# A transformer-like kernel on one core: all hi one-hots of the expert scatter move from GpSimd to DVE, with new orders for PE, ACT and GpSimd and new PSUM banks

## What is computed

```python
x = _L0_conv_ref(x, ...)                 # per image: layernorm, q; strided 7x7 depthwise conv gives offsets;
                                         # bilinear sampling of x at 64 places; 8-head attention; MLP
t = _to_tokens(x)
t = t + _L1_attn_ref(_ln_t(t), ...)      # 8 heads, top 4 of 16 segments of 32 keys per query
t = t + _L1_ffn_ref(_ln_t(t), ...)       # experts chosen by product keys:
#   q  = layernorm(t @ Wq.T + bq) per head (8 heads of 64); two halves, l2norm
#   s0, s1 = scores against 64 + 64 keys; top 16 of each
#   fs, pos = top 16 of the 16 x 16 sums; ci = ix0 + ix1 is the expert (0..126)
#   inner = t . expert_down[fi]; out = sum(gelu(inner) * softmax(fs) * expert_up[fi])
```

## Time and profile before

| | |
|---|---|
| Three runs | 449.9, 451.67 (median), 452.0 us |
| The profiled execution | 449.87 us, its span 447.8 us |
| DVE busy | 358.4 us, 80% |
| PE busy | 308.1 us, 69% |
| POOL busy | 217.9 us, 49% |
| ACT busy | 140.7 us, 31% |
| Mean granted PE clock | 0.701 |

### The profile page before, as it was taken

One profiled execution on the slowest core, in us unless ns is written; L12 is line 12 of the kernel. 1 busy time (PEld: TensorE's weight loads), 2 busy tenths in 40 slices (PEclk: granted clock), 3 DMA queues, 4 the chain that ended last, 5 costly groups with the idle time before them and its releaser, 6 DMA issues.

```text
span 447.8 us, 7841 instructions
## 1 busy us (share of the span) xinstructions
PE 308.1 (69%) x2275; PEld 225.2 (50%) x2275; DVE 358.4 (80%) x2163; ACT 140.7 (31%) x324; POOL 217.9 (49%) x411
## 2 busy tenths in 40 slices
PE   2096558788119576799978778996556769850497
PEld 1044235456016344498855457974323359730494
DVE  1848238238999989799999979999997899999930
ACT  2125231655213147523224373033042241041000
POOL 6319932227935387796244937312073532085700
PEclk9997566898655678865685986568659576566556
DMA  6000000000000000000000000000000000000000
GB/s 222 0 0 1 1 1 0 1 1 1 1 1 0 1 2 1 1 1 1 2 1 1 1 13 1 2 0 3 1 1 12 0 1 2 2 0 12 2 1 12
DMA packets 1634, 3.50 MB, mean 8 GB/s; under 512 B 180, under 2 KB 1205, under 8 KB 1592
## 3 DMA queue, kind: packets, MB, share of 16 engines
q1 hardware_dynamic: 1592, 3.01, 1.9%
HBM read 2.49 MB, written 0.52 MB: 7 GB/s over the span
## 4 chain that ended last, share of the span: by engine, by line
DVE 55%; PE 23%; POOL 9%; issue 6%; ACT 6%; DMA 1%; DVEq 0%; ACTq 0%; POOLq 0%
PE bank L876 6%; DVE Sx L1363 5%; DVE i L1369 5%; DVE i L1370 5%; DVE cands L1419 4%; DVE onehot L494 4%; DVE vraw L1366 3%; DVE vraw L1360 3%; DVE segmax L1244 3%; DVE c L1416 3%; PE bank L540 2%; PE bank L550 2%; DVE masked L1426 2%; PE bank L783 2%; ACT hat L914 2%
## 5 line engine op out<-in xcount | busy, mean ns | idle before, releaser
L876 PEld LDWEIGHTS bank<-weights,onehot 108*128 108x128 f16 x1024 | 69.0, 178 | 3.1 <-DVE onehot L494 1.5
L876 PE MATMUL bank<-weights,onehot 108*128 108x16 f16 x1024 | 69.0, 216 | 1.9 <-DVE onehot L494 1.4
L1644 POOL TENSOR_TENSOR inv<-nrm,mhalf 128x16 f32<-128x16 f32 x8 | 23.4, 2925 | 35.8 <-DVE nrm L1376 35.8
L458 POOL TENSOR_TENSOR taps<-qpad,wa 128x128 f32<-128x128 f32 x96 | 36.0, 427 | 2.0 <-ACT qpad L929 1.9
L540 PE MATMUL bank<-wa,hat 128*128 128x128 f32 x24 | 6.7, 371 | 32.9 <-ACT hat L914 32.9
L1557 POOL TENSOR_TENSOR rstd<-veps,mhalf 128x2 f32<-128x2 f32 x16 | 11.7, 731 | 34.6 <-DVE veps L1166 34.3
L1370 DVE FIND_INDEX8 i<-vraw,Sx 128x8 uint16<-128x64 f32 x128 | 28.0, 219 | 0.0
L1369 DVE FIND_INDEX8 i<-vraw,S 128x8 uint16<-128x64 f32 x128 | 28.0, 218 | 0.0
L1363 DVE MATCH_REPLACE8 Sx<-vraw,S 128x64 f32<-128x64 f32 x128 | 25.1, 209 | 0.0
L803 PE MATMUL bank<-KB,qsT 128*128 128x256 f32 x64 | 24.9, 558 | 0.2 <-issue 0.2
L494 DVE TENSOR_SCALAR onehot<-eT 108x512 f16<-108x512 uint16 x84 | 24.4, 366 | 0.0
(11 more groups left out here) (228 smaller groups left out, 811.5 us busy)
## 6 DMA issues: line engine op xcount, KB each, us to landing
wa<-wa_dram SPq DMA_DIRECT2D x1, 747.5 KB, 4.9
wb<-wb_dram SPq DMA_DIRECT2D x1, 707.0 KB, 5.2
x_sb<-x_dram SPq DMA_DIRECT2D x4, 128.0 KB, 4.0
out_dram<-eT SPq DMA_DIRECT2D x4, 128.0 KB, 1.7
onehot<-ws_dram SPq DMA_DIRECT2D x1, 448.0 KB, 5.9
bq_row<-rows_dram SPq DMA_DIRECT2D x1, 0.5 KB
onehot<-rows_dram SPq DMA_DIRECT2D x1, 13.5 KB
```

The costliest lines, as they stand in the source:

```text
L458: ins = eng.tensor_tensor(tv[:, :, :, ky, kx:kx + n], q, dw[:, ky, kx:kx + n].unsqueeze(1).unsqueeze(1).broadcast_to([P, G8, G8, n]), ALU. ...
L876: last = mm(o[:, g * 16:g * 16 + 16], OHv[:, c * NT + t, g], Rv[:, c, t, g, s], start=(c == 0 and s == 0), stop=(c == NCH - 1 and s == 1))
L1644: g_.tensor_tensor(inv[:, n], nrm[:, n], mhalf[:, 0:2 * H], ALU.pow).then_inc(inv_ready, 1)
```

## The change

All 32 one-hots are DVE's. POOL's N3b and N3i and the semaphore onehot_pool_ready are gone. The orders of PE, ACT and POOL and the banks are new; DVE's order is the same. PE has 19 fillers in place of 21, at other places. In POOL's order only N3b and N3i are taken out. In the orders, cut to the parts spoken of below:

```diff
-POOL_HI = 4
...
     "tensor":
-    A1a.0 A2d.0 A1b.0 W.0 W.1 A3a.0 A3b.0 A3c.0 A4.0 W.2 W.3 F5a.0 A1a.1 F5c.0 NS.0 F6a.0 F6b.0 W.4 W.5
-    F6c.0 F7a.0 F7b.0 F8a.0 A1b.1 F8b.0 F9b.0 A2d.1 F9a.0 F9c.0 A3a.1 A3b.1 W.6 A3c.1 A4.1 W.7 W.8 F8c.0
-    F9d.0 W.9 F10a.0
+    A1a.0 A1b.0 A2d.0 A3a.0 A3b.0 A3c.0 A4.0 F5a.0 A1a.1 A1b.1 F5c.0 F6a.0 W.0 NS.0 F6b.0 F6c.0 F7a.0 F7b.0
+    F8a.0 W.1 W.2 F8b.0 F9b.0 F9a.0 A2d.1 F9c.0 A3a.1 A3b.1 A3c.1 A4.1 W.3 W.4 F9d.0 F8c.0 F10a.0
...
-    A4.2 F11a.1 F11t.1 F5a.2
+    F11a.1 A4.2 W.6 W.7 F11t.1 F5a.2
...
-    F11a.3 N6b.1 F11t.3 W.12 W.13 F11b.3 F11c.3 W.14 N3a.2 F12.3 N0a.3
+    F11a.3 F11t.3 W.10 W.11 N6b.1 F11b.3 F11c.3 W.12 N3a.2 W.13 W.14 W.15 W.16 F12.3 N0a.3
...
-    N5a.2 N0f.3 N0e.3 W.15 N5b.2 N0g.3 W.16 N6a.2 W.17 N4.3 N6b.2 N3a.3 N3h.3 N5a.3 W.18 N5b.3 W.19 W.20 N6a.3 N6b.3
+    N5a.2 W.17 N5b.2 W.18 N4.3 N6a.2 N6b.2 N3a.3 N3h.3 N5a.3 N5b.3 N6a.3 N6b.3
     "scalar":
-    F5b.0 A1a.1 F5c.0 F6b.0
+    F5b.0 A1a.1 A1b.1 F5c.0 F6b.0
...
-    F12.0 F5c.1 N0a.0 F6b.1 A1a.2 N0h.0 N0b.0 N0c.0
+    F12.0 F5c.1 N0a.0 N0h.0 F6b.1 N0b.0 N0c.0 A1a.2
...
-    F12.1 N4.0 F5c.2 N0a.1 N0h.1 A0b.3
+    F12.1 F5c.2 N0a.1 N4.0 A0b.3 N0h.1
...
-    N4.2 N0e.3 N2p.3 N2q.3 N6a.2 N4.3 N3a.3 N3h.3 N6a.3
+    N4.2 N0d.3 N0e.3 N6a.2 N2p.3 N2q.3 N3a.3 N3h.3 N4.3 N6a.3
...
@@ PE @@
             def N5a(b):
                 pe.wait_ge(onehot_dve_ready, b + 1)
-                pe.wait_ge(onehot_pool_ready, b + 1)
                 scatter(b, 0)
...
@@ DVE @@
             def N3b(b):
-                for hi in range(POOL_HI, HI):
+                for hi in range(HI):
                     last = masks(v, hi, first_halves(b))
                 last.then_inc(onehot_dve_ready, 1)
...
@@ POOL @@
-            def N3b(b):
-                if b >= 1:
-                    full(pool, "G1", b - 1)
-                pool.wait_ge(eT_ready, b + 1)
-                for hi in range(0, POOL_HI):
-                    last = masks(g_, hi, first_halves(b))
-                last.then_inc(onehot_pool_ready, 1)
```

More of the change, by code:

```diff
@@ L109 @@
 ORDERS = {
-    "tensor": """A1a.0 A2d.0 A1b.0 W.0 W.1 A3a.0 A3b.0 A3c.0 A4.0 W.2 W.3 F5a.0 A1a.1 F5c.0 NS.0 F6a.0 F6b.0 W.4 W.5
-        F6c.0 F7a.0 F7b.0 F8a.0 A1b.1 F8b.0 F9b.0 A2d.1 F9a.0 F9c.0 A3a.1 A3b.1 W.6 A3c.1 A4.1 W.7 W.8 F8c.0
[L112 to L129, removed]
+    "tensor": """A1a.0 A1b.0 A2d.0 A3a.0 A3b.0 A3c.0 A4.0 F5a.0 A1a.1 A1b.1 F5c.0 F6a.0 W.0 NS.0 F6b.0 F6c.0 F7a.0 F7b.0
+        F8a.0 W.1 W.2 F8b.0 F9b.0 F9a.0 A2d.1 F9c.0 A3a.1 A3b.1 A3c.1 A4.1 W.3 W.4 F9d.0 F8c.0 F10a.0 F10b.0
+        F11a.0 W.5 F11t.0 F5a.1 F11b.0 F11c.0 A1a.2 F5c.1 F12.0 N0a.0 F6a.1 N0h.0 F6b.1 N0b.0 F6c.1 N0c.0 N0f.0
+        N0d.0 F7a.1 F7b.1 N0e.0 F8a.1 F8b.1 N0g.0 F9b.1 F9a.1 A1b.2 F9c.1 A2d.2 F8c.1 A3a.2 F9d.1 A3b.2 A3c.2
+        F10a.1 F10b.1 F11a.1 A4.2 W.6 W.7 F11t.1 F5a.2 F11b.1 F11c.1 N3a.0 N4.0 F5c.2 F12.1 N0a.1 N0h.1 W.8
+        F6a.2 A1a.3 W.9 F6b.2 N0b.1 F6c.2 N0c.1 N0d.1 N0f.1 N5a.0 F7a.2 N0e.1 F7b.2 N5b.0 F8a.2 F8b.2 A2d.3
+        F9b.2 F9a.2 F9c.2 N0g.1 F8c.2 N6a.0 A1b.3 F9d.2 A3a.3 F10a.2 A3b.3 F10b.2 A3c.3 F11a.2 N4.1 A4.3 F11t.2
+        F5a.3 F11b.2 N6b.0 F11c.2 N3a.1 F5c.3 F12.2 N0a.2 N0h.2 F6a.3 F6b.3 N0b.2 F6c.3 N0c.2 N0f.2 N5a.1 N5b.1
+        F7a.3 N0d.2 F7b.3 N0e.2 N0g.2 F8a.3 F8b.3 F9b.3 F9a.3 F9c.3 N6a.1 F9d.3 N4.2 F10a.3 F10b.3 F8c.3 F11a.3
+        F11t.3 W.10 W.11 N6b.1 F11b.3 F11c.3 W.12 N3a.2 W.13 W.14 W.15 W.16 F12.3 N0a.3 N0h.3 N0b.3 N0c.3 N0f.3
+        N0d.3 N0g.3 N0e.3 N5a.2 W.17 N5b.2 W.18 N4.3 N6a.2 N6b.2 N3a.3 N3h.3 N5a.3 N5b.3 N6a.3 N6b.3""".split(),
@@ new lines @@
+    "scalar": """A0b.0 A1a.0 A2c.0 A2d.0 A1b.0 A3a.0 A3b.0 A3c.0 A4.0 A0b.1 F5b.0 A1a.1 A1b.1 F5c.0 F6b.0 F7a.0 F7b.0
+        F8a.0 A2c.1 F8b.0 A2d.1 F9a.0 A3a.1 A3b.1 A3c.1 F8c.0 A4.1 F10a.0 F10b.0 A0b.2 F11t.0 F11b.0 F5b.1 F12.0
+        F5c.1 N0a.0 N0h.0 F6b.1 N0b.0 N0c.0 A1a.2 F7a.1 N0d.0 F7b.1 N0e.0 F8a.1 F8b.1 N2p.0 A2c.2 F9a.1 A2d.2
+        A3a.2 F8c.1 A3b.2 A1b.2 N2q.0 A3c.2 F10a.1 F10b.1 F11t.1 A4.2 F11b.1 N3a.0 F5b.2 F12.1 F5c.2 N0a.1 N4.0
+        A0b.3 N0h.1 F6b.2 N0b.1 A1a.3 N0c.1 N0d.1 F7a.2 N0e.1 F7b.2 F8a.2 A2c.3 F8b.2 A2d.3 N2p.1 F9a.2 F8c.2
+        A3a.3 N6a.0 F10a.2 A3b.3 F10b.2 A1b.3 N2q.1 A3c.3 F11t.2 A4.3 F11b.2 F5b.3 N3a.1 F12.2 F5c.3 N0a.2 N0h.2
+        F6b.3 N0b.2 N0c.2 N4.1 F7a.3 N0d.2 F7b.3 N0e.2 F8a.3 F8b.3 N2p.2 F9a.3 F10a.3 F10b.3 N6a.1 F8c.3 N2q.2
+        F11t.3 F11b.3 N3a.2 F12.3 N0a.3 N0h.3 N0b.3 N0c.3 N4.2 N0d.3 N0e.3 N6a.2 N2p.3 N2q.3 N3a.3 N3h.3 N4.3
@@ L141 @@
         A2b.1 F8b.3 F7b.0 A2b2.1 A3a.1 A4.1 A0a.2 A0b.2 F11c.0 N0a.0 N0h.0 A2a.2 F6c.1 A2a2.2 A2b.2 A2b2.2 N0f.0
[L142 to L145, removed]
+        F7b.1 N2a.0 N0g.0 A3a.2 N2d.0 N2c.0 A4.2 N2f.0 F11c.1 A0a.3 A0b.3 N0a.1 N0h.1 A2a.3 F6c.2 A2a2.3 A2b.3
+        N0f.1 A2b2.3 F7b.2 N2a.1 A3a.3 N0g.1 N2d.1 A4.3 N2c.1 N2f.1 F11c.2 N0a.2 N0h.2 F6c.3 N0f.2 F7b.3 N2a.2
+        N2c.2 N0g.2 N2d.2 N2f.2 F11c.3 N0a.3 N0h.3 N0f.3 N0g.3 N2a.3 N2d.3 N2c.3 N2f.3""".split(),
 }
@@ L155, in schedule @@
     return out
[L158 to L161, removed]
+BANKS = """01234560132456013245601234560123452160163405234160523416052163462142314263052463
+         01524630152563015234601523460152341352605134023460512345162350164235601042352614
+         35261435206135213065126302563254106354120654143206514326143261430261430621406235
+         46210356201"""
 def place_jobs():
@@ L404, in build @@
         onehot_dve_ready = sem("onehot_dve_ready")
-        onehot_pool_ready = sem("onehot_pool_ready")
         out_ready = sem("out_ready")
@@ L865, in N5b @@
                     pe.wait_ge(onehot_dve_ready, b + 2)
-                    pe.wait_ge(onehot_pool_ready, b + 2)
                 scatter(b, 1)
@@ L1120, in N3a @@
                     ac.wait_ge(onehot_dve_ready, b)
-                    ac.wait_ge(onehot_pool_ready, b)
                     full(ac, "YT", b - 1)
@@ L1700, in N2f @@
                 merge(b, 1)
-            def N3b(b):
-                if b >= 1:
-                    full(pool, "G1", b - 1)
-                pool.wait_ge(eT_ready, b + 1)
-                for hi in range(0, POOL_HI):
-                    last = masks(g_, hi, first_halves(b))
-                last.then_inc(onehot_pool_ready, 1)
[L1710 to L1714, removed]
             do = {"A0a": A0a, "A0b": A0b, "A2a": A2a, "A2a2": A2a2, "A2b": A2b, "A2b2": A2b2, "A3a": A3a, "A4": A4, "F6c": F6c, "F7b": F7b,
                   "F11c": F11c, "NS": NS, "N0a": N0a, "N0h": N0h, "N0f": N0f, "N0g": N0g, "N2a":
-                  N2a, "N2c": N2c, "N2d": N2d, "N2f": N2f, "N3b": N3b, "N3i": N3i}
+                  N2a, "N2c": N2c, "N2d": N2d, "N2f": N2f}
             for s, b in schedule("gpsimd"):
```

## The result

The changed kernel took 444.5 us (median of 4 runs, 442.65 to 446.63) against 451.84 us (449.9 to 452.19) for the kernel before: ratio 0.9864, 95% interval [0.9833, 0.9895]. It is faster by 1.4%. The profiled execution took 442.65 us, its span 440.9 us, where before's took 447.8: 6.9 us less.

A forecast was written before the change was run, and what follows sets the result against it. DVE was taken to bound the kernel from about 105 to 429 us, a dependent chain before, PE after. Terms -5.6 - 1.0 - 1.46 + 0.5 - 0.6 + 0.3 + 0.8 = -7.1 us gave 444.5 us, range 439.5 to 449.5.

The forecast's parts named there:

- Port relief, images 0 to 2: DVE's 32 one-hots per image run faster with POOL quiet than 28 beside it: 5.6 us saved.
- rival D: Full blocking: each POOL one-hot stops DVE for its whole length, so relief is 16.1 us, total 434 us; chance 0.03.
- Tail one-hots: Image 3: 32 one-hots of 256 columns on DVE take 4.58 us instead of 5.59, 1.0 us saved.
- Tail fillers: PE fillers W.18 to W.20 leave the order around the last scatters: 1.46 us saved.
- The late exponential: Tail of image 3: ACT's N6a.2 ahead of N2p.3 delays the exponential and POOL's queue: 0.5 us lost, bounds 0 and 2.
- The seam of image 1: A4.2 and two fillers come ahead of F11t.1: 0.3 us lost, up to 1.
- I count 1.1 of the 1.52: Image 0: DVE's shorter work then waits for POOL's inverse root, so 1.1 of 1.52 us gained is kept.
- The seam of image 3: Fillers W.12 to W.16 about N3a.2 hold PE's clock for the queries: 0.6 us saved; 1.0 gained to 1.5 lost.
- The front: Image 0: new PE and ACT order, A1b.1 before F5c.0, outcome depending on PE's clock: 0.8 us lost.
- C: Slower: PE's full clock from 80 to 108 us is lost, costing 9.2 us, in all 453.8 us; chance 0.06.
- B: Seams, front and ACT's late exponential give back about half of the gain: 447 to 449.4 us; chance 0.17.
- E: No relief: slow one-hot step has another cause; 454.6 to 456.6 us, half relief 449.5 to 451.5; chance 0.12.

The follow-up runs named there:

- e3: Changed kernel with POOL again building four one-hots, into a tile nobody reads, ACT's N3a waiting for them; ratio 1.0054 to the kernel before.
- e4: Kernel before without the tail fillers W.18, W.19 and W.20; ratio 0.9982.
- e9: Kernel before, its orders and banks kept, with all one-hots on DVE and without tail fillers W.18 to W.20; 442.17 us, ratio 0.9826.
- e10: Kernel before, its orders and banks kept, with all one-hots on DVE, run once more as base; ratio 0.9851 to the kernel before.
- e5: Changed kernel with ACT's N6a.2 put back behind N2p.3 and N2q.3; ratio 0.9845 to the kernel before.
- e11: Changed kernel with ACT's N6a.2 behind N2p.3 and N2q.3, a second run of that edit; ratio 0.9870 to the kernel before.
- e2: Kernel before with the changed kernel's PE and ACT orders and banks, one-hots still split 28 on DVE and four on POOL; ratio 1.0013.
- e1: Kernel before, its orders and banks kept, with all 32 one-hots on DVE and none on POOL; ratio 0.9846.
- e8: Changed kernel run again unchanged, as base on the same chip; ratio 0.9871 to the kernel before.
- e6: Changed kernel without the seam fillers W.8, W.9 and W.12; ratio 0.9889 to the kernel before.
- e7: Changed kernel without W.8, W.9 and W.12 and with ACT's N6a.2 behind N2p.3 and N2q.3; ratio 0.9860 to the kernel before.

## Why the prediction was right

444.5 us was forecast and 444.5 measured, inside the range. The main step was right in mechanism and size, as far as the one-hots themselves go. Several small terms were not, and they cancel; this close a hit is partly luck. In the profiled pair the span fell by 6.9 us: -5.96 by the one-hots of images 0 to 2, +1.47 of that given back at the seam of image 1, +0.34 there by the orders, -0.38 at the seam of image 3, +1.50 on the way to its one-hots, -1.17 by these, -1.15 by the tail fillers, -1.64 in the front; 0.1 is rounding and small shifts. The front came 2.4 us better than its term; the way to image 3's one-hots and the seam of image 1 came about 1 us worse each. By the steps of the sum:

**Port relief, images 0 to 2: right in the groups, not all kept.** Forecast per image 1.52 (with the masks and products of image 0), 2.04 and 2.45 us; measured from the groups 6.82, 8.58 and 8.99 down to 6.55, 6.56 and 6.56, with 1.30 and 3.33 down to 0.89 and 2.50: 1.51, 2.02 and 2.43. The step of 0.202 us, read in the earlier trace rows where POOL had just stopped, priced instructions that did not exist yet to 0.02 us a group. e3 shows the other price: 32 cost 9.39 us in image 1. If POOL slows DVE until its fourth is done, the slow step of 0.365 us follows from the earlier trace rows, and (9.39 - 6.56) / (0.365 - 0.202) = 17 of the 32 ran at it, against 18 in the earlier trace rows.

The rule of the Trainium skill, SBUF — State Buffer, "Who interferes with whom" (an exclusive lock that blocks the loser for the whole instruction of the other), was weighed as rival D. In image 1 of e3 DVE's longest one-hot was 0.695 us beside instructions of 1612 to 1761 ns on POOL, and the group lost 2.83 us, not 6.2. That the two engines hurt each other holds, the size does not.

**Tail one-hots: right.** -1.0 forecast, 5.59 to 4.42 is -1.17. The step was taken as 0.141 us and is (4.42 - 0.22) / 31 = 0.135.

**Tail fillers: right, forecast -1.46.** The stretch behind N3b.3 is 1.51 us shorter in e4, 1.40 in e9 against e10, and 1.15 in the profiled pair.

**The late exponential: the step that was sized too small.** "Price 0.5 us; bounds 0 and 2." The chain was as described, and it cost 0.97 us, by e5 and e11 against the changed kernel. The forecast counted the queue of POOL up to 410.8 without slowdown. In the trace POOL's cells of t = 1 and the merge ran beside DVE's instructions and stretched: five products at line 1655 took 2.37 us, where 1.55 is usual, and seven at line 1670 took 2.85, where most such groups take 1.95. The wait that came of it is 2.37 us; against e5, DVE's own work is 1.4 us shorter where POOL stands idle, and so the cost is 0.97.

A further 0.5 us of this stretch is there with an early exponential too, under either orders (52.74 in e10, 52.72 in e5, 52.18 before). DVE waits for nothing in it. POOL's merge of t = 1 moved to where its one-hots had been, as forecast, but the forecast gave that no price: DVE's masks and products there take longer beside the merge than beside POOL's one-hots. Before, and then e10:

```profile
412.59 0.92 DVE L1469 TENSOR_SCALAR cands<-eT 108x256 f16<-108x256 uint16 x4
413.54 2.04 DVE L1479 TENSOR_TENSOR weights<-W,cands 108x256 f16<-108x256 f16 x8
```

```profile
406.69 1.23 DVE L1466 TENSOR_SCALAR cands<-eT 108x256 f16<-108x256 uint16 x4
407.95 2.26 DVE L1476 TENSOR_TENSOR weights<-W,cands 108x256 f16<-108x256 f16 x8
```

**The seam of image 1: another wait than forecast.** The forecast was a loss of 0.3 us by the orders and, of image 0's relief of 1.52 us, 0.42 not kept because DVE waits for POOL's inverse root. Measured is a seam longer by 1.81 us. e2 splits it: it has the changed kernel's orders, its front (103.76 and 103.74) and its clock of 0.50 from 176 to 188 us, and its seam is 9.13. So 0.34 us comes from the orders, as forecast. The other 1.47 us is all that image 0 had gained. F6a.2 starts at 180.46 on PE in both traces; DVE, done 1.5 us sooner, waits 2.03 us for it in the changed kernel and, in e2:

```profile
183.96 0.26 DVE L1198 RECIPROCAL rec<-bank 128x16 f32<-128x16 f32 x1 [0.53 <-PE bank L634]
```

The first top-k of image 1 starts at 191.77 in e2 and 191.73 after. e3 and e11, whose orders differ only in the tail, are a second such pair (195.42 and 195.40). With the old orders the seam takes back less: 0.49 us in e1 and 0.48 in e10, of 1.48 and 1.46. The term "I count 1.1 of the 1.52" so fits the old orders; in these two pairs under the new ones nothing was kept, and the wait is PE's F6a.2.

The clock has a part in this. e4, with the old order, had 0.50 in the same window too, and its seam was 9.64 us, against 8.79, 9.28, 9.27 and 9.23 in the others of the old order at 0.78 and more. e5 and e11 are one kernel; e5 had 0.77 and a seam of 8.23 us, e11 0.61 and 10.63. So the seam moves by 2.4 us in one and the same kernel, more than between the orders. Most of it is lost again, however: the next stretch is 84.31 us in e5 and 82.60 in e11, and the two together differ by 0.7.

**The seam of image 3: the wait went as forecast, the gain did not.** W.12 to W.16 were to save 0.6 us by holding the clock; 0.38 was measured. The two queries take 1.12 or 1.13 us each in all eight traces with the new orders, and in all five with the old ones at least one takes 1.74 or more. In e2 the waits for the squares and the inverse root are 0.24 and 0.61 us, against 0.31 and 1.65 for squares alone before. But ahead of that DVE waits 1.75 us for the copied slots, against 1.05, behind a PE order that now has W.12 before N3a.2, and 2.21 us before the product at line 1271, against 1.82: the whole stretch is 85.78 us in e2 and 85.76 before. e10, with the old orders, has 82.25, shorter than the changed kernel's 82.95; its first query ran in 1.13 us without them. So these fillers save nothing in sum. What W.13 to W.16 do alone was not tested.

**The front: +0.8 forecast, -1.6 in the profiled execution, about +0.7 over several.** The prediction had two branches: F6a.0 at half clock, the key copies near 46.7; or at full clock, and z 1.8 us earlier. The profiled execution fell into the second, but z, at 49.81 before, came only 0.7 us earlier. PE's and DVE's timelines of after:

```profile
42.15 1.94 PE L631 MATMUL bank<-vBD,PT 128*128 128x34 f32 x16 [0.79 <-ACT PT L980]
```

```profile
44.86 0.92 DVE L1313 COPY KB<-bank 32x64 f32<-32x64 f32 x4
...
49.07 0.42 DVE L1201 TENSOR_TENSOR z<-bank,x_sb 128x256 f32<-128x256 f32 x1 [2.48 <-PE bank L645]
```

e8, the same kernel, fell into the first, with z 1.4 us late and not 1; the windows' row, then DVE's timeline:

```profile
42.00:43.00 1.00, 0.86 (x5) 0.89 (x5) 0.96 (x2) 0.04 (x1) 1.00 (x2) 0.50 0.00 0
```

```profile
47.00 0.92 DVE L1313 COPY KB<-bank 32x64 f32<-32x64 f32 x4 [2.30 <-PE bank L536]
...
51.20 0.42 DVE L1201 TENSOR_TENSOR z<-bank,x_sb 128x256 f32<-128x256 f32 x1 [2.48 <-PE bank L645]
```

Of the eight traces with the new orders (after, e2, e3, e5 to e8, e11), three have 1.94 us for F6a.0 and key copies at 44.8 to 44.9, five have 3.60 us and 47.0. Their first top-k starts at 103.65 to 107.77, on average 105.86; in the five with the old orders (before, e1, e4, e9, e10) at 104.33 to 106.18, on average 105.16. The forecast's +0.8 is about the difference of these means, 0.7, though with eight and five executions this is an estimate. The new order spreads wider (4.1 us against 1.9) and gains nothing on average; which of its moves does that, A1b.1 before F5c.0 or another, was not tested.

**The rivals.** C did not come: in all thirteen traces the windows from 88 to 106 us read 1.00. B is partly true. The seam of image 1 and the late exponential did give back 1.8 and 1.0 us, and in an execution like e8 the front does too. It did not decide: of the relief of 5.96 us, 4.5 was left behind the seam. D and E are refuted by e3 and by the groups of 32.

## What to carry to other kernels

When two engines share a piece of work, look in the trace for the moment at which one of them stops: the step of the other before and after that moment prices the split, and here DVE alone did 32 one-hots faster than DVE did 28 beside POOL's four. Then ask at each place which wait comes next: a shorter group is worth only what that wait leaves, and in image 0, under the new orders, it left nothing in two pairs of traces. Test such a change without its new orders: the one-line part carried the whole gain, and the rewritten orders were worth nothing. A wait that depends on PE's clock should be given two branches with a price each, and compared over several executions; a microsecond read in one pair of traces is not a gain.

## What the runs showed of the hardware

- **The slowdown also hits other forms.** Beside POOL's one-hots, DVE's products of two fp16 tiles took 3.32 us for four, against 2.50, and its masks 1.31 against 0.89 (e3, and the same in the earlier trace rows). POOL in turn slowed beside DVE (2.85 for 1.95 us, line 1670).
- **Twice, POOL was held up for the whole of DVE's row.** In e4, image 2, POOL's inverse root began at 353.16, just before DVE's 28 one-hots, and ended at 359.38, as they did at 359.35. It took 6.22 us for 1.77 before at the same place, and DVE ran as if alone: 5.75 us, where 28 x 0.202 + 0.07 is 5.73. POOL's timeline of e4:

```profile
353.16 6.22 POOL L1633 TENSOR_TENSOR qrstd<-ssq,mhalf 128x8 f32<-128x8 f32 x1 [0.57 <-DVE ssq L1328]
354.77 10.58 POOL L494 TENSOR_SCALAR onehot<-eT 108x512 f16<-108x512 uint16 x4
```

and DVE's:

```profile
353.60 5.75 DVE L494 TENSOR_SCALAR onehot<-eT 108x512 f16<-108x512 uint16 x28
```

  In e11, image 1, where POOL had no one-hots at all, the second of two inverse roots ended at 278.05, as DVE's 32 one-hots did at 278.00; it took 7.28 us:

```profile
269.17 8.88 POOL L1626 TENSOR_TENSOR qrstd<-ssq,mhalf 128x8 f32<-128x8 f32 x2 [5.39 <-DVE ssq L1321]
```

  Here POOL does look locked out, but through 28 and 32 instructions of DVE, and not for one, as the Trainium skill, SBUF — State Buffer, "Who interferes with whom", has it. Who is slowed was seen to differ between executions with the same instructions at this place; what decides it stays open. In e4 DVE then waited 1.50 us for PE and 2.43 for ACT in the top-k of image 3, and the 3.2 us saved were lost again before the one-hots.
- **Durations and the granted clock can disagree.** In e3, e6, e7 and e11 F6a.0 took 3.60 us, as in e8, where the row reads 0.50; but in these four the row from 42 to 46 us reads 1.00, as it would at full clock, where F6a.0 took 1.94 us. Durations are the safer witness there.
- **Executions of one kernel lie 4 us apart and more** (442.65 to 446.63 for the changed one, 441.59 to 447.60 for e7). Between e5 and e11, one kernel, the profiles show where: of 4.4 us the front has 3.7, and the seam of image 1 with the stretch behind it 0.7.
